# In the first chunk of a graph layer, the ring of adjacency blocks is filled one step sooner

## The reference, cut to what matters

```python
def _L0_gnn_ref(x, adj, W1, b1, W3, b3, Wf, bf):
    h = jax.nn.relu(adj @ (x @ W1) + b1)
    h = jax.nn.relu(adj @ (h @ W3) + b3)
    return jnp.tanh(h @ Wf + bf)

x = x + _L0_gnn_ref(_layernorm(x), adj, ...)     # x: 2048 x 256, adj: 2048 x 2048, float32
x = x + _L0_ffn_ref(_layernorm(x)[None], ...)[0]  # 8 experts, the best 2 of each row, hidden width 1024
```

## The kernel before, in words

| engine | order in step s |
|---|---|
| TensorE | transposes of x tile s+2; z1_rows(s+1); product(s) |
| ScalarE | hi_of_block(s); x_sub and roots; (in step 4, the issue of three DMAs that write zero rows); copy x_T(s+2); z1_hi(s+1) |
| VectorE | lo_of_block(s); x_T_lo(s+2); x_norm; z1_lo(s+1); the turns of the step |

## Time and profile before

### The profile page before, as it was taken

How to read it: one execution, slowest core, us unless ns; L and a number is a source line. 1 busy time by engine, 2 the same in 40 slices (tenths; PEclk the granted TensorE clock), 3 DMA queues, 4 the chain that set the end, 5 groups by cost and what they waited for, 6 DMA issues and landing times.

```text
span 616.0 us, 11115 instructions
## 1 busy us (share of the span) xinstructions
PE 577.4 (94%) x3248; PEld 491.1 (80%) x3249; DVE 373.5 (61%) x804; ACT 296.3 (48%) x561; POOL 144.8 (24%) x143
## 2 busy tenths in 40 slices
PE   2878999999999999999989999999999999999993
PEld 2766777787877877779878988988989889898873
DVE  5888878884666797567743333346333735566671
ACT  2654554565656484567423323354233635465461
POOL 3000000000000506036654233232222231222222
PEclk9999999999999999999999999999999999999998
DMA  9999990000212764431047222126211623646722
GB/s 200 225 224 215 215 215 17 0 1 0 104 35 68 145 179 166 137 104 19 2 77 256 37 36 33 22 34 221 34 26 26 189 68 79 183 97 167 221 34 28
DMA packets 66419, 63.73 MB, mean 103 GB/s; under 512 B 5914, under 2 KB 60828, under 8 KB 66364
## 3 DMA queue, kind: packets, MB, share of 16 engines
q1 hardware_dynamic: 57724, 52.32, 34.7%
q0 software_dynamic: 8224, 10.53, 10.5%
q10 hardware_dynamic: 432, 0.39, 0.2%
HBM read 54.02 MB, written 10.26 MB: 104 GB/s over the span
## 4 chain that ended last, share of the span: by engine, by line
PE 76%; DVE 9%; issue 5%; ACT 5%; DMA 3%; POOL 1%; SPq 1%; POOLq 0%; ACTq 0%; DVEq 0%
PE bank L1625 27%; PE bank L1651 14%; PE bank L1496 8%; PE bank L1498 7%; PE bank L1497 7%; PE bank L1679 4%; PE bank L1525 2%; DVE ring L978 2%; PE bank L1509 2%; DVE adj_s L1016 2%; DMA adj_s<-in_adj 1%; PE bank L1618 1%; ACT ring L648 1%; PE bank L1522 1%; ACT hTf L660 1%
## 5 line engine op out<-in xcount | busy, mean ns | idle before, releaser
L1625 PE MATMUL bank<-ew,xeT 128*128 128x512 f32 x840 | 202.2, 395 | 1.9 <-DVE ew L1333 1.4
L1625 PEld LDWEIGHTS bank<-ew,xeT 128*128 128x128 f32 x840 | 154.6, 188 | 33.4 <-issue 2.3
L1496 PE MATMUL bank<-ring,Z 128*128 128x512 f32 x256 | 104.4, 408 | 13.5 <-DVE ring L978 13.2
L1651 PE MATMUL bank<-ew,heT 128*128 128x256 f32 x840 | 109.1, 286 | 3.5 <-issue 2.4
L978 DVE TENSOR_TENSOR ring<-adj_s,ring 128x512 fp32r<-128x512 f32 x128 | 86.1, 682 | 39.4 <-ACT ring L648 38.2
L1651 PEld LDWEIGHTS bank<-ew,heT 128*128 128x128 f32 x840 | 102.9, 191 | 5.2 <-issue 3.7
L1498 PE MATMUL bank<-ring,Z 128*128 128x512 f32 x256 | 100.1, 391 | 0.0
L1497 PE MATMUL bank<-ring,Z 128*128 128x512 f32 x256 | 100.1, 391 | 0.0
L648 ACT CAST ring<-adj_s 128x512 fp32r<-128x512 f32 x128 | 76.8, 624 | 39.5 <-PE bank L1498 27.8
L522 POOL DMA_INDIRECT slot_rows<-val,route x32 | 36.2, 1130 | 206.7 <-issue 202.7
L555 POOL DMA_INDIRECT out<-y_st,idx_st x29 | 45.4, 1564 | 160.2 <-ACT y_st L806 153.4
(11 more groups left out here) (189 smaller groups left out, 557.8 us busy)
## 6 DMA issues: line engine op xcount, KB each, us to landing
w_raw<-in_L_ffn_W SPq DMA_DIRECT2D x24, 1024.0 KB, 5.7
adj_s<-in_adj SPq DMA_DIRECT2D x64, 256.0 KB, 6.3
x_in<-in_x SPq DMA_DIRECT2D x16, 128.0 KB, 5.7
x_res<-in_x SPq DMA_DIRECT2D x4, 512.0 KB, 3.6
out<-x SPq DMA_DIRECT2D x4, 512.0 KB, 4.3
ffn_in_rows<-x_res SPq DMA_DIRECT2D x4, 512.0 KB, 4.2
xg<-ffn_in_rows,idx POOLq DMA_INDIRECT x39, 3.0
Wg<-in_L_gnn_W SPq DMA_DIRECT2D x2, 256.0 KB, 3.3
```

The source lines that it names most:

```text
L1496: nc.tensor.matmul(a, zh, hi, start=(jb == 0), stop=False)
L1625: last = nc.tensor.matmul(out_ap, stat[:, sl, k, :], w_at(k, wl), start=(k == k0 and sl == wl == 0), stop=(k == k1 - 1 and sl == 1))
L1651: last = nc.tensor.matmul(y_p[:, 0:D], heT[:, sl, k, :], ew[:, o + 2 * H * wl + D * k:][:, 0:D], start=(k == sl == wl == 0), stop=(k == KH ...
```

## The change

On ScalarE and VectorE, block 0 is cast and subtracted ahead of the loop. In step `s` of the first chunk both engines take the copy (or the low part) of x tile `s + 2` first, and then block `s + 1` instead of block `s`; from step 16 on they take block `s` as before. The order on TensorE does not change. Two entries of `turned_before` go up: 12 turns stand ahead of step 7 (11 before), and 16 ahead of step 11 (15 before), since block 8 is now cast in step 7 and block 12 in step 11.

```diff
@@ scalar @@
             z1_hi(0)
+            hi_of_block(0)
             for s in range(2 * S1):
                 layer, c, jb = s // S1, s % S1 // NT, s % NT
-                hi_of_block(s)
+                if s < NT - 2:
+                    x_T(s + 2)
+                if s < NT - 1:
+                    hi_of_block(s + 1)
+                if s >= NT:
+                    hi_of_block(s)
...
                 if s < NT - 1:
-                    if s < NT - 2:
-                        x_T(s + 2)
                     z1_hi(s + 1)
@@ vector @@
-                early = (4, 4, 6, 8, 8, 8, 10, 11, 12, 13, 14, 15)
+                early = (4, 4, 6, 8, 8, 8, 10, 12, 12, 13, 14, 16)
...
             z1_lo(0)
+            lo_of_block(0)
             for s in range(2 * S1):
                 layer, c, jb = s // S1, s % S1 // NT, s % NT
-                lo_of_block(s)
+                if s < NT - 2:
+                    x_T_lo(s + 2)
+                if s < NT - 1:
+                    lo_of_block(s + 1)
+                if s >= NT:
+                    lo_of_block(s)
                 if layer == 1 and first_expert_at(c, jb):
                     first_lo(*first_expert_at(c, jb))
-                if s < NT - 2:
-                    x_T_lo(s + 2)
                 if s < NT - CT and s % CT < 3:
                     x_norm(1 + s // CT, s % CT)
```

## The result

| | before | changed |
|---|---|---|
| median us | 618.52 (618.01 to 619.16, 4 runs) | 612.84 (612.19 to 614.39, 4 runs) |
| span of the profiled execution | 616.0 | 610.3 |

The ratio is 0.9911, 95% interval 0.989 to 0.9933. The forecast was 614.3 with a range of 612.8 to 616.6; the median lies inside its lower edge by 0.04 us. Every ratio compares fast runs alone; only w3_pool, further down, had slow ones, two of ten at 626 us. Two more comparisons of the same two kernels, each on another chip, gave 0.9937 (0.9913 to 0.9961) and 0.993 (0.9906 to 0.9953). The forecast's 4.3 us is a ratio of 0.9930.

A forecast was written before the change was run, and what follows sets the result against it. VectorE's nearly full line of work starves TensorE in the first chunk; 38.9 us of work plus 1.8 idle after 14.84 releases product 15 at 55.5 instead of 59.8, so 618.58 - 4.3 = 614.3 us, range 612.8 to 616.6.

The forecast's parts named there:

- The bound: First chunk, 14.8 to 59.8 us: TensorE starves, products wait 9.9 us for low parts of blocks; VectorE is nearly full.
- The sum of VectorE's work, 38.9 us and 1.8 idle: First chunk, up to product 15's release: VectorE work plus remaining idle time ends z1_lo(15) at 55.5 us, 4.3 us sooner.
- The waits for copies of x and for z vanish: VectorE, first chunk: 2.3 us of waits for x copies fall to nearly nothing, z's 1.4 us likewise.
- The check of the steps: VectorE work between products covers the copy's 2.31 us: least 2.52 us (steps 4 and 0), all others 2.6 or more.
- The turn less ahead of product 15, 0.6 us: VectorE, end of first chunk: z1_lo(15) releases product 15, so the sixteenth turn falls behind it, gaining 0.6 us.
- What comes late, the turns at blocks 4, 8 and 12: Steps 3, 7, 11: casts wait for turns just made; VectorE stays idle 0.49 us three times, 1.5 us.
- The table of turns: Two turns pulled forward by a step, needed by the new order; a smaller edit priced at nothing, none outrunning its load.
- The chain behind product 15: hidden1 and the low part of block 20 follow product 15 at fixed distances, so the 4.3 us arrive whole.
- TensorE's wait for line 978 under 1 us, and 4 to 5 us of new waits on z: Expected trace sign: TensorE's waits for low parts of blocks shrink, small new waits for low parts of z (line 971) appear.
- Late copies: Rival, first chunk: the 2.3 us of waits for x copies stay, gain 2.0 us, 616.6 us; chance 0.10.
- The slower case: Rival: waits for x copies grow at the head of 14 steps by 0.6 us each, 4.1 slower, 622.7 us; chance 0.04.
- VectorE held to full durations: Rival: VectorE instructions take their full duration, leaving no idle time to give back; no change, 618.6 us; chance 0.04.

The follow-up runs named there:

- w3_pool: Changed kernel with the split of W3 on GpSimd instead of VectorE; 618.1 us, ratio 0.9922 against the kernel before.
- The doubled low parts: Low-part subtraction of blocks 2 to 13 run twice on VectorE: changed kernel 621.99 us, ratio 1.0072; kernel before 622.82 us, 1.0085; both ratios against the kernel before.
- turns_sooner: Changed kernel with the last turns of each group of four one step sooner still; 614.61 us, ratio 0.9951 against the kernel before.
- z_first: Changed kernel, but in steps 3, 7 and 11 ScalarE and VectorE take z tile s+1 ahead of block s+1; 617.66 us, ratio 0.9912 against before.
- scalar_only: Kernel before with the changed kernel's ScalarE order and turn table, VectorE's order left as before; 619.94 us, ratio 0.9996 against before.

## Why the prediction was right, point by point

**The bound.** Right. TensorE starved for low parts, and VectorE's line of work, nearly full, set the chunk. The doubled low parts show it: 6.6 of 6.8 us arrive in the changed kernel, 4.2 before.

**The sum of VectorE's work, 38.9 us and 1.8 idle.** Right to within a tenth: 40.71 us measured from the first low part to the end of z1_lo(15), 40.7 forecast. The idle terms, from start to start, were 0.47 three times instead of 0.49, and 0.16 and 0.18 at steps 1 and 5 instead of 0.15 (the low part of block 2 starts 0.50 after that of the x tile, where 0.34 is the unbroken distance). The prediction added rounded terms; unrounded they make 38.8, which changes nothing here.

**The waits for copies of x and for z vanish.** Right where the first matmuls are 0.23 us apart: none is left. Where it is 0.43, one stays, 1.38 us at step 1, which belongs to the slow first products, and behind it 0.2 us for a high part of z. The check of the steps was not complete, though: it put every step but two at 2.6 us of cover or more, while step 3 in front of step 4 and step 7 in front of step 8 make 1.21 + 0.34 + 0.57 + 0.40 = 2.52 too, with the idle time at blocks 4 and 8 on top. These are the two steps at which turns_sooner found its waits.

**The turn less ahead of product 15, 0.6 us.** The timeline has it, 15 turns instead of 16 up to the release of product 15. It is part of the 4.25 that were found and was not tried alone.

**What comes late, the turns at blocks 4, 8 and 12.** Right, and z_first shows the price of leaving it: 1.3 us by the traces, with the allowance made there.

**The table of turns** was costed as a condition of the new order only. Alone it gives 1.3 us. The sum was right nonetheless, because it counted idle time left over and not the gain of each edit; read as a split by edits, it would have been wrong.

**The chain behind product 15.** Right: hidden1, h_lo and block 20 followed at their distances. Product 20 starts at 63.53 against 68.10: 4.57, which is the 4.15 of product 15 and the 0.39 of the first load to within 0.03.

**TensorE's wait for line 978 under 1 us, and 4 to 5 us of new waits on z.** The first holds only without the 2.0 us in front of product 0, which I had overlooked in the row of 9.9. The second was too high: 2.8 us.

**The size at the end.** 4.3 forecast, 5.7 measured. The surplus was not a term of the change: 0.39 us of a load that landed sooner and 1.2 us at the slot lists, which other traces of either kernel have or lack. The comparisons at 0.9937 and 0.993 lie around the forecast of 0.9930. So the mechanism was right, and that the first median stayed inside the range, by 0.04 us, was luck. What the prediction missed is how much the time spreads behind the chunk, 6 us in the same code; 0.2% was too fine a bound for it.

**The rivals.** Late copies: not in this kernel, but turns_sooner is that rival made real, and it cost what the sooner turns had brought. The slower case: in the changed kernel a wait of 0.31 us or more at the head of a step came only with the slow first products. VectorE held to full durations: excluded, VectorE is busy for 38.5 of the 40.5 us from 14.8 to product 15, where it was busy for 39.9 of 45.0 before, and its instructions start as close as before. The prediction gave half of what the Trainium skill, "VectorE: DVE Perf Modes", section "The DRAIN you can't avoid", says: the same section goes on that a next operation that is not held starts earlier. With that half the trace agrees, by 0.57 us from start to start for a low part listed at 0.65.

## What to carry to other kernels

When one engine is nearly full and another starves behind it, add up the full engine's work from start to start over the whole stretch and price an order by the idle time it leaves, rather than by the waits that it removes: here that sum held to a tenth of a microsecond. An operation that must wait for something just made belongs behind one that need not, and work taken out of a light step has to leave the cover that the next transfer or copy in the loop needs. In a kernel whose later stages spread by more than the gain, compare the stretch in the traces, at the same speed of the matmuls.

## What the runs showed of the hardware that was not expected

TensorE's first products run at two speeds from one execution to the next of the same code, and the row of the granted clock mostly doesn't tell. In the second trace of the changed kernel the matmuls of 128x512 from 15.89 to 21.17 us are 0.43 us apart with 1.00 in the clock row, later 0.23. In seven of the nine traces with 0.43 the row stays at 1.00. In scalar_only, where it does tell (as in z_first), the stretch reads so (us; PE, PEld, DVE, ACT, POOL busy; clock; DMA share; GB/s):

```profile
16.00:17.00 1.00, 1.00 (x4) 0.81 (x4) 0.93 (x6) 0.00 (x0) 0.00 (x0) 0.65 1.21 212
17.00:18.00 1.00, 1.00 (x5) 0.70 (x5) 0.91 (x2) 0.00 (x0) 0.00 (x0) 0.50 1.18 238
...
20.00:30.00 10.00, 8.74 (x51) 7.16 (x50) 8.34 (x22) 5.17 (x13) 0.00 (x0) 1.00 1.20 223
```

0.50 is the lower of the two levels, 1.2 GHz. That the seven with 1.00 in the row ran at it too is inferred from the same distance of 0.43 us. In front of product 0 TensorE waits for the first quarter of the adjacency and what follows from it. That idle time was 1.85, 1.99, 2.03, 2.08 and 2.12 us in the five executions with 0.23 us between the first matmuls, and 2.08, 2.18, 2.42, 2.51, 2.54, 2.69, 2.69, 2.72 and 2.74 in the nine with 0.43, in part or in full. So a first load that lands some tenths later seems to cost its delay and then up to 1.9 us more; the two groups meet at 2.08, and no run set that idle time on purpose, so the cause is not shown.
